# Cross attention on one core: the row maximum subtracted inside the transposed score product, the clip moved behind the exponential

## The reference

```python
q = (query @ Wq + bq).reshape(B, Nq, H, D).transpose(0, 2, 1, 3)
k = (key_value @ Wk + bk).reshape(B, Nkv, H, D).transpose(0, 2, 1, 3)
v = (key_value @ Wv + bv).reshape(B, Nkv, H, D).transpose(0, 2, 1, 3)
attn = jnp.einsum('bhqd,bhkd->bhqk', q, k) * scale
attn = jnp.clip(attn, -CLAMP, CLAMP)              # CLAMP = 10000
attn = jax.nn.softmax(attn, axis=-1)
x = jnp.einsum('bhqk,bhkd->bqhd', attn, v).reshape(B, Nq, Cq)
return x @ Wo + bo
```

## Time and profile before

| | us |
|---|---|
| median of three runs | 868.16 |
| the three runs | 868.16, 860.56, 869.66 |
| span of the profiled execution, first to last instruction | 862.7 |
| of it, layer 0 | 0 to about 254 |
| of it, `attention1` | about 255 to 475 |

### The profile page before, as it was taken

The page is one execution under the profiler, slowest core; times in us unless marked ns, Lnnn a source line. Parts: engine busy times, 40 slices in busy tenths (PEclk is TensorE's granted clock), DMA queues, the critical chain, the costliest instruction groups (busy, mean ns, idle before and its releaser), DMA issues. The chain is left out here.

```text
span 862.7 us, 26300 instructions
## 1 busy us (share of the span) xinstructions
PE 727.4 (84%) x10112; PEld 545.5 (63%) x10112; DVE 639.6 (74%) x1802; ACT 408.4 (47%) x777; POOL 198.2 (23%) x317
## 2 busy tenths in 40 slices
PE   3468898888888889889999477887759999999997
PEld 2245565555556777667787245665547888888886
DVE  7568877787868989888996577887665766666653
ACT  3123223322235656656655365665635555554553
POOL 3333222232534212330200553342011110011100
PEclk9569989998898999999999599999998999999999
DMA  4000000140034221122200000000000000000000
GB/s 103 9 22 13 23 21 21 33 88 18 24 99 100 82 78 50 53 66 79 81 15 14 4 2 5 5 4 4 5 3 2 13 13 0 12 12 12 12 13 13
DMA packets 33082, 26.43 MB, mean 31 GB/s; under 512 B 9740, under 2 KB 29912, under 8 KB 32984
## 3 DMA queue, kind: packets, MB, share of 16 engines
q1 hardware_dynamic: 29944, 24.07, 10.5%
q10 hardware_dynamic: 3040, 0.98, 0.5%
HBM read 13.51 MB, written 7.34 MB: 24 GB/s over the span
## 5 line engine op out<-in xcount | busy, mean ns | idle before, releaser
L1931 PEld LDWEIGHTS bank<-w2r,hme 128*128 128x128 f32 x1024 | 132.2, 191 | 15.6 <-ACT hme L1876 1.4
L1931 PE MATMUL bank<-w2r,hme 128*128 128x128 f32 x1024 | 135.5, 276 | 0.0
L1876 ACT ACTIVATE hme<-bank,b 128x512 f32<-128x512 f32 x128 | 86.5, 687 | 96.3 <-PE bank L97 96.3
L984 ACT ACTIVATE P<-bank 128x512 f32<-128x512 f32 x128 | 76.6, 598 | 76.2 <-PE bank L1130 75.0
L1900 DVE SCALAR_TENSOR_TENSOR Xq<-bank,wgte,Xq 128x128 f32 (+1 forms) x256 | 72.1, 344 | 51.1 <-PE bank L1931 38.3
L1056 DVE TENSOR_SCALAR bank<-bank 128x512 f32<-128x512 f32 x128 | 89.6, 700 | 15.2 <-PE bank L1121 14.4
L1064 DVE TENSOR_REDUCE mx<-bank 128x4 f32<-128x512 f32 x128 | 87.1, 681 | 1.4 <-PE bank L1104 1.3
L500 ACT ACTIVATE w2r<-bank 128x512 f32<-128x512 f32 x40 | 23.9, 597 | 114.5 <-PE bank L814 82.8
L1130 PE MATMUL bank<-mT,negsel 128*128 128x128 f16 x512 | 51.0, 223 | 13.9 <-DVE bank L1056 12.6
L95 PE MATMUL bank<-xTe,w 128*128 (+1 forms) x128 | 48.8, 381 | 5.5 <-PEq L1295 5.5
L825 PE MATMUL bank<-w_raw,hm 128*128 128x128 f32 x320 | 50.3, 308 | 2.9 <-DVE X L739 2.8
(11 more groups left out here) (382 smaller groups left out, 1785.3 us busy)
## 6 DMA issues: line engine op xcount, KB each, us to landing
cross_q<-qh SPq DMA_DIRECT2D x24, 128.0 KB
...
```

The costliest lines, as they stand in the source:

```text
L984: act.activation(P[j][:], TB[u % 3][:], ACT.Exp, scale=SCALE).then_inc(s["p_ready"], 1)
L1876: act.activation(hm[:, p % HR], UP[p % RING][:], ACT.Gelu_apprx_tanh, bias=b1[:, p:p + 1]).then_inc(s["gelu"], 1)
L1931: last = pe.matmul(Y[f % 2][:, cols], hm[:, p % HR, cols], w2r[:, p], start=(p % 2 == 0 and i == 0), stop=(p % 2 == 1), skip_group_check=True)
```

## The change

The maximum is no longer subtracted by a product of its own. `m16` is laid out as four blocks of 32 columns, with the maxima of unit j in column j of a block; four transposes (`turn_max`) put them into 32 rows, and ACT copies them (128x128 before, 32 rows by 512 columns now) into rows 96 to 127 of `Q`. Rows 96 to 127 of `K` now hold -1 in row 96+j of unit j and 0 elsewhere, written once by GpSimd (`negative_rows`): for `K[0]` in layer 0 in group 0, behind the root of group 1, and for `K[1]` at the start of `attention1`. So `score_t` gives the score less its maximum. The exponential gets a bias from a tile `shift`, and the clip is applied to the result in SBUF (`P[j]`), between a least value and 1. `score_t(b, 0)` now waits for the maxima in `Q`; `less_max`, `negsel`, `mT` and the semaphores `t_clip` and `t_neg` are gone. The order of the four streams is shifted: on PE the units run one slot later (score_t(b-1,3) in the first slot of step b, behind `turn_max(b)`), on DVE the maxima go ahead of the clips, on ACT the copy of the maxima goes ahead of the exponential of (b-1,3).

```diff
+def negative_rows(pool, K, ident):
+    for j, t in enumerate(K):
+        last = pool.tensor_scalar(t[KEY_ROWS:128, :], ident[KEY_ROWS:128, KEY_ROWS + j:KEY_ROWS + j + 1].broadcast_to([32, 16 * S]),
+                                  -1.0, 0.0, ALU.mult, ALU.add)
+    return last
...
             def step(g):
                 for p in range(NBLK):
+                    if isinstance(g, int) and g == 0 and p == 1:
+                        pool.wait_ge(s["rsB"], 2)
+                        negative_rows(pool, c["K"][0], ident).then_inc(cs["neg_rows"], 1)
+                        pool.wait_ge(cs["neg_rows"], 1)
...
-                elif t == 4:
-                    dve.tensor_scalar(c["negsel"][:], ident[:, 0:NH].unsqueeze(2).broadcast_to([128, NH, 128]), -1.0, None,
-                                      ALU.mult)
...
             for t in K[1]:
-                last = pool.memset(t[:].bitcast(mybir.dt.uint32), 0)
+                last = pool.memset(t[0:KEY_ROWS].bitcast(mybir.dt.uint32), 0)
             last.then_inc(s["zeros"], 1)
+            pool.wait_ge(s["zeros"], 2)
+            negative_rows(pool, K[1], ident).then_inc(s["neg_rows"], 1)
+            pool.wait_ge(s["neg_rows"], 2)
...
-                act.activation(P[j][:], TB[u % 3][:], ACT.Exp, scale=SCALE).then_inc(s["p_ready"], 1)
+                act.activation(P[j][:], TB[u % 3][:], ACT.Exp, bias=c["shift"][:], scale=SCALE).then_inc(s["p_exp"], 1)
...
+                if has(b):
+                    act.wait_ge(s["mT_psum"], b + 1)
+                    q = Q[n % 2][KEY_ROWS:128, :].rearrange("r (h i q) -> r h i q", h=4, i=4)
+                    act.activation(q[:, :, i, :], M.rearrange("r (h q) -> r h q", h=4), ACT.Copy).then_inc(s["mT_ready"], 1)
                 if has(b - 1):
                     exp(b - 1, U - 1)
-                if has(b):
-                    act.wait_ge(s["mT_psum"], b + 1)
-                    after(act, s["t_neg"], U * b)
-                    act.activation(mT[:], M.bitcast(F16), ACT.Copy).then_inc(s["mT_ready"], 1)
...
             def clip(b, j):
                 if has(b):
-                    dve.wait_ge(s["t_psum"], U * b + j + 1)
-                    dve.tensor_scalar(TB[(U * b + j) % 3][:], TB[(U * b + j) % 3][:], -CLIP, CLIP, ALU.max, ALU.min
-                                      ).then_inc(s["t_clip"], 1)
+                    dve.wait_ge(s["p_exp"], U * b + j + 1)
+                    dve.tensor_scalar(P[j][:], P[j][:], LEAST, 1.0, ALU.max, ALU.min).then_inc(s["p_ready"], 1)
...
             def step(b):
+                maxima(b + 1, 0)
+                clip(b - 1, 3)
+                maxima(b + 1, 1)
                 clip(b, 0)
-                maxima(b + 1, 0)
+                prepare(b // 4, b % 4)
+                maxima(b + 1, 2)
                 clip(b, 1)
-                maxima(b + 1, 1)
-                prepare(b // 4, b % 4)
-                clip(b, 2)
-                maxima(b + 1, 2)
-                clip(b, 3)
                 maxima(b + 1, 3)
...
+                clip(b, 2)
...
-            def less_max(b, j):
-
-                pe.wait_ge(s["mT_ready"], b + 1)
-                pe.wait_ge(s["t_clip"], U * b + j + 1)
+            def turn_max(b):
+
+                pe.wait_ge(s["m_ready"], b + 1)
+                after(pe, s["mT_ready"], b)
                 for h in range(4):
-                    last = pe.matmul(TB[(U * b + j) % 3][:, cols(h)], negsel[:, 4 * j + h, :], mT[:],
-                                     start=False, stop=True, skip_group_check=True)
-                last.then_inc(s["t_neg"], 1)
+                    last = pe.transpose(M[:, cols(h)], m16[:, 32 * h:32 * h + 32], ident16[:])
+                last.then_inc(s["mT_psum"], 1)
```

63 lines of the change are left out of this document (35 added, 28 removed).

## The result

The changed kernel takes 875.6 us (median of 4 runs, 872.34 to 877.47); the kernel before, on the same chip, 864.95 us (860.56 to 869.66). The ratio is 1.0115, with a 95% interval of 1.0061 to 1.0169: slower by about 1.1%, where 857 us were forecast. The profiled execution has a span of 875.3 us, against 862.7 before.

The account below looks back on a forecast made before the run. The prediction took DVE's own work, with 0.4 us of waits, to bound an ordinary step, turning into a chain through all engines. Its terms, -26 + 6 + 4 + 6 = -10 us, gave 857 us, range 842 to 875.

Parts of the forecast that it names:

- The steps, minus 26: `attention1`: 28 steps take 160.8 us for 183.8, minus 23; the four steps outside bring it to minus 26.
- the chain: Ordinary step: turn, copy, exponential, clip, values, `OE`, preparation, next exponential, clip, last maxima and `m16` in sequence, 5.6 us.
- the 12 us put down for GpSimd: `attention1`: plus 6 for clips held by GpSimd's normalisation and plus 6 for clips held by the rows of K.
- a PE that waits in `turn_max`: Sign against the forecast: PE waiting at the turn of the maxima for longer than 0.5 us a step.
- the ring: The forecast's chain through all engines, from one `m16` to the next in an ordinary step of attention, 5.6 us.
- the first step: First step of a chunk: DVE waits for ACT's half of x, then works 1.8 us; 7.35 us in all.
- GpSimd holding the clips, plus 6: `attention1`: some three SBUF clips wait in each of five GpSimd normalisations, 1.2 us, small constants add a little; plus 6.
- Rows of K in layer 0, plus 4: Layer 0: four GpSimd operations of 3.1 us fit an idle gap but hold one `xnB` operation; plus 4.
- dear-price rival: Rows of K at 5.8 us an operation, holding `xnB` in layer 0 and clips in `attention1`: 876 us, chance 0.2.
- Rows of K in attention, plus 6: Start of `attention1`: the rows of `K[1]` alternate with the first clips, three waits of 2.5 us, less idle time; plus 6.
- Behind the loop, taken as nothing: After the attention steps: no term in the sum; `negsel` going, 1.2 us of DVE near the end, counted as nothing.
- The chain is longer by its hops: Attention step: 0.1 us in each of eleven hops, 1 us a step; 867 us, chance 0.2 shared with an unshortened clip.

Follow-up runs that it names:

- e7: The changed kernel with the turn of the maxima ahead of the next step's first score product on TensorE; 876.6 us.
- e8: e7 plus a second move on TensorE: the transposes of the outputs go behind the values of units 0 and 1; 879.0 us.
- e9: The changed kernel with unit 1 clipped behind `m16`, the turn behind the values of unit 0, and unit 1's values with units 2 and 3; 869.3 us.
- e18: e14 with the changed kernel's own order of clip, maxima and turn put back; 861.6 us.
- e14: e9 with rows of -1 behind layer 0's normalisation, chunk statistics in the preceding chunk's last step, and shorter GpSimd row copies and memsets; 850.1 us.
- e13: The changed kernel with each GpSimd operation that writes the rows of -1 cut into two halves; 873.4 us.
- e2: The changed kernel without rows of -1 in layer 0 or attention, tiles zeroed whole, maximum not subtracted; 870.7 us.
- e15: The kernel before with a chunk's statistics taken in the last step of the preceding chunk; 858.7 us.

## Why the prediction was wrong

It was wrong in sign: 857 us forecast, 842 to 875 the range, and 875.6 measured. The miss against the profiled span is 22.6 us (852.7 forecast, 875.3 found): 15.2 between the first and the last `m16`, 4.65 ahead of them, 2.75 behind.

**The steps, minus 26: the failed step is the first of the chain.** For the 28 steps 160.8 us were forecast and 184.8 found. A third of the 24 us are slow steps, below; the other 16.3 us are 0.58 a step in the mean. (That the whole stretch missed by only 15.2 us is because the 12 us put down for GpSimd in it were mostly not spent.) Put beside the forecast, the timeline of a last step shows where (times from the end of `m16`, at 318.12):

| | forecast | found |
|---|---|---|
| turn of the maxima begins | 0 | 0.51 |
| copy begins | 0.48 | 0.94 |
| exponential (b,3) begins | 0.96 | 1.55 |
| its clip ends | 2.11 | 2.70 |
| ScalarE's preparation begins | 3.1 | 3.74 |
| exponential (b+1,1) begins | 3.65 | 4.22 |
| its clip begins | about 4.4 | 4.94 |
| `m16` ends | 5.6 | 6.17 |

Everything from the exponential on came at the distances forecast. The turn was put at zero, as if TensorE stood ready; it was in its transposes, values and the next score product, behind a wait of 0.71 us for ScalarE's copy of Y. Where the turn was not late, at 305.87 us, the step took 5.73 us, 0.13 over the forecast. The rest is the spacing of copy and exponential, 0.61 us for 0.48. The text named the fear ("a PE that waits in `turn_max`"), but looked for the wait at the wrong end: TensorE did not wait in the turn, the turn waited for TensorE. e7 showed the queue (0.33 us a step); e8 and e9 showed that the ring has a second side, clip (b,1) ahead of the last maxima. That second side was in the forecast chain; what was not drawn from it is that it could be reordered away, for 11.5 us (e18 against e14).

**Steps slow by themselves: 7.7 us, not in the sum.** Two second steps at clocks of 0.77 and 0.58, 3.3 us over 5.73; the second step of attention, 2.6; the step with the memsets, 1.8 over its like. The mean clock of 0.98 in the earlier trace rows hid that the kernel before has two steps of 7.6 to 7.7 us among its second steps as well. The forecast gave the first step 7.35 us; it kept 7.96 of its 8.25, with as much of TensorE's work in it as before (6.1 us for 6.0).

**GpSimd holding the clips, plus 6: right for memsets, wrong for the normalisation.** Over the whole span a clip takes 426 ns in the median; three clips exceed 1 us, 1.03 and 1.73 beside GpSimd's rows and 2.30 beside the memset. Among the 79 from 284 to 415 us, which the normalisations of four chunks overlap, the longest is 604 ns (single line, then the timeline, in which a clip starts inside such an operation and runs through it):

```profile
L1076 DVE TENSOR_SCALAR P<-P x79: 409/426/604, 284.5 to 414.8; 128x512 f32<-128x512 f32 x79
```

```profile
334.65 0.93 POOL L196 TENSOR_SCALAR xn<-X,mv,rs 128x128 f32<-128x128 f32 x1
...
335.02 0.42 DVE L1076 TENSOR_SCALAR P<-P 128x512 f32<-128x512 f32 x1
```

All five normalisations cost the clips 0.3 us in sum (58.6 us of clips, less 128 x 0.426, less 3.8 us for the three). The rule that whoever comes first keeps the ports for a whole instruction (the Trainium skill, SBUF — State Buffer, "SBUF: two separate sides") agrees with `xnB` and with the memset of `Kd`, and does not agree with these clips: here the measurement decides. Why GpSimd's normalisation does not hold them is open.

**Rows of K in layer 0, plus 4: the price was too high, the count too low.** An operation costs 1.90 us, not 3.1, close to the lower bound of 1.8 taken from the fills. The estimate of about 1.8 that was worked out from the Trainium skill's GPSIMD Engine Reference ("Engine selection") agrees with it. But "one is held for up to 3.1 us" counted one of four operations of `xnB`. All four waited, 4 x 1.7 = 6.8 us; e13, with operations of half the length, showed the turns. The same text says "clip and GpSimd alternate" for attention; the rule was known and not applied to the place where four operations stand in a row. At 1.90 us the dear-price rival was out; the forecast was overtaken by the count.

**Rows of K in attention, plus 6: some 2.6.** The first two steps take 17.65 us, and 15.02 without rows (e2): 2.6 us, since one clip and `m16` were held for 1.3 and 1.0 us and another clip for 0.6.

**Behind the loop, taken as nothing: 2.7 us, open.** From the last `m16` to the end the two kernels with the old order of VectorE have 399.0 and 400.9 us (before, e15), the others 401.7 to 407.1. The tail of attention accounts for 0.9 us of it in the changed kernel. In the second attention the single rounds change (16 to 19 us each), but from the first to the last of its rounded maxima it takes as long as before (133.6 us for 133.5), so the remaining 1.8 us lie behind it. No run tells whether they are the change's doing.

**The rivals.** The time of 876 given for the dear price was met, by another mechanism: GpSimd's operations cost less than the forecast's. "The chain is longer by its hops" was nearest in kind, with 6.1 us a step forecast and 6.17 found, and was given only 867 us because it held the losses to GpSimd at zero but for 4 and knew nothing of the slow steps. Its own terms did not give that number either: 2 x 0.26 us more in 32 steps take 16.6 us off the 26, not 21, and with 4 in layer 0 the time would have been some 863.

**What the loss against the kernel before is made of.** Of the 12.6 us between the two spans 8.65 lie ahead of the loop, where `xnB` accounts for 6.8; in attention the first two steps lose 2.1 and the step with the memsets 1.8, which the other steps win back but for 1.2 in all; 2.7 lie behind. The ring of 6.17 us is why nothing was won in the loop, not where the loss itself lies.
